# The two weight products of a graph layer, as three 16-bit products of high and low parts

## The chip, the cores and the metric

The kernel runs on one core of a Trainium2 chip. The metric is device time in microseconds (us) of one execution of the whole kernel, the median of several runs.

## What is computed

Input are 625 rows of 768 values, 20,000 edges between the rows, and the weights of a graph network of two attention layers and of one transformer block with eight experts. Only the first graph layer matters here. Cut to that:

```python
x0  = layernorm(x)                          # 625 x 768
xl  = (x0 @ W1).reshape(625, 4, 256)        # W1: 768 x 1024   "xl1"
e   = leaky_relu(alpha_src[src] + alpha_dst[dst], 0.2)   # alpha: sums of xl with a row per head
out = segment_sum(xl[src] * softmax_over_edges_into_dst(e), dst) + b1
h   = relu(layer_norm(out)) + (x0 @ Wr1 + br1)           # Wr1: 768 x 1024   "res1"
```

All of it is float32. The softmax over edges is done densely: an edge count matrix, 625 x 625, says how often each source reaches each target, and log(count) is added to the scores.

## The kernel before, in words

The 625 rows are five tiles (T = 5) of P = 125 rows, numbered t, or d where they are targets of edges. 768 is KD = 6 blocks of 128, HC = 1024 is two banks of 512. Each engine has its own program, in order; they meet at semaphores. TensorE's outputs go to four PSUM slots of 1024 columns in the order of `item_plan`: product n may start when the owner of product n-4 ("A" ScalarE, "D" VectorE) has emptied it (`free`, `done`, `emptied_by`).

*Start.* SyncE loads the edges, x, W1 and Wr1 (3072 KB each, one DMA each, L465 and L466), then rows of biases and small columns (L468 to L474), one DMA after the other. VectorE takes the moments of each tile (L1021), GpSimd the inverse root (L591, L592), VectorE normalizes (L1038), TensorE transposes (L1507), and ScalarE (tiles 0, 2, 4) or VectorE (tiles 1, 3) copies the transpose to `aT6` in float32 (L753, L1073).

*Count loop.* For each d, TensorE makes xl1 of tile d (12 float32 products of 512 columns, L1519), then sums the edge counts: the edges are sorted by target and come in groups of 500, of which 8 to 10 touch a tile (44 in all, so the loop has a length read from a register). Per group TensorE does 4 pairs of float16 products, 512 and 113 columns (L1557, L1558), with one-hot rows that are built on the fly in a ring of 4 groups (`oh_dst`, `oh_src`). VectorE builds a group with one comparison of 4 x 125 columns (L1105) and three of 625 (L1108); ScalarE builds the fourth source row in two steps, the absolute difference to `distance` (L774), and relu(1 - distance) (L779), one buffer between them. VectorE and ScalarE may be 4 groups ahead of TensorE (`oh_used`). For the next d they start when TensorE has left this count. VectorE first takes the sums of `xl1` with the attention rows (L1091, eight of 256 columns) and copies the counts out (L1115, L1119). GpSimd clamps the counts at 1 (L598), ScalarE takes the logarithm (L786), GpSimd makes the mask (L601).

*Attention.* 20 steps i (4 heads x 5 tiles), a pipeline over ScalarE (L837, exponential L842, copy of the transpose L753), VectorE (L1152, L1155, result L1177) and TensorE (transpose, product of 256 columns in float32). Between them TensorE does halves of res1 as `RES1_HALVES` says: tile 0 before the first step and in step 0, then (tile, half) (1,0) (1,1) (2,0) (2,1) in steps 1, 13, 15, 18, and tiles 3 and 4 behind the last step. W2 of the second layer is loaded at the end of the count loop and split into float16 high and low parts by ScalarE (L798) and VectorE (L1139), a half in step 7 and one in step 11 (`SPLIT_AT`). Behind it VectorE adds up each row tile (L1207, L1210, L1215), TensorE transposes it and multiplies by W2 and Wr2, already in the form "three products of float16 parts": high x high, high x low, low x high (`PARTS`, L1621 and L1519).

The rest (second layer, attention with 12 heads, experts) is not touched but for where buffers lie.

## Time and profile before

| | |
|---|---|
| median of 3 runs | 1099.87 us (1098.56 to 1102.97) |
| the profiled execution's own time | 1102.97 us, span 1101.2 us |
| TensorE busy | 1037.7 us, 94% of the span |
| VectorE, ScalarE, GpSimd busy | 729.8, 570.8, 184.9 us |
| granted TensorE clock, mean over the span | 0.978 |

The span is the time from the first to the last instruction of the profiled execution; it was also the slowest of the three runs. In the profile PE is TensorE's products, PEld its weight loads, DVE VectorE, ACT ScalarE, POOL GpSimd, SP SyncE. A line number is that of the statement that issued the instruction, and that can be a helper's: L1519 stands for all of `product`, L753 for all of `copy`. A duration of a product counts its way through the array, so a row of products is read by the distance of starts or by a merged row's length, not by the mean of one.

### The profile page before, as it was taken

To read this page: it belongs to the slowest core of one execution; us is meant where nothing else is said; L and a number is where in the kernel's file an instruction comes from. 1 tells how busy PE (TensorE), PEld (TensorE's weight loads), DVE (VectorE), ACT (ScalarE), POOL (GpSimd) and SP (SyncE) were. 2 spreads that over 40 slices of the span, in tenths; PEclk is the share of its full clock that TensorE was granted. 3 is DMA by queue.
4 is the path that set the end of the run, shared out by engine and by line. 5 is a ranking of instruction groups with operands and counts; after the bars stand their busy time and mean duration, and the time that the engine had idled before them with its cause. 6 is when DMAs were issued, how large, how long until landed. Compare 5 with 4: busy or idle time off the path is not lost.

```text
span 1101.2 us, 19073 instructions
## 1 busy us (share of the span) xinstructions
PE 1037.7 (94%) x6167; PEld 651.7 (59%) x6168; DVE 729.8 (66%) x1300; ACT 570.8 (52%) x782; POOL 184.9 (17%) x186
## 2 busy tenths in 40 slices
PE   5999999999999999989998699999999999999997
PEld 3555558756766775566777255555555555555554
DVE  6677768595666654189976888911129898989411
ACT  2666769513240344178834576811128778777310
POOL 3000040040205331072001301110103120211000
PEclk9999999999999999989998699999999999999999
DMA  8300030301507500030026699940009999999100
GB/s 312 106 0 0 1 115 1 115 1 59 112 1 156 87 1 1 1 112 2 2 86 201 244 390 325 351 168 0 25 0 352 375 375 360 390 359 390 72 4 3
DMA packets 92263, 155.60 MB, mean 141 GB/s; under 512 B 36507, under 2 KB 36587, under 8 KB 92214
## 3 DMA queue, kind: packets, MB, share of 16 engines
q1 hardware_dynamic: 89814, 149.20, 39.2%
q0 software_dynamic: 2400, 5.77, 1.5%
q8 instruction: 29, 0.48, 0.2%
q14 instruction: 20, 0.16, 0.0%
HBM read 153.21 MB, written 7.77 MB: 146 GB/s over the span
## 4 chain that ended last, share of the span: by engine, by line
PE 75%; DVE 10%; issue 5%; ACT 4%; DMA 2%; POOL 1%; DVEq 1%; SPq 0%; ACTq 0%; POOLq 0%
PE psum L1519 29%; PE psum L1794 18%; PE psum L1769 17%; PE psum L1778 2%; PE psum L1507 2%; PE psum L1557 2%; DVE area L1380 2%; DMA low<-in_L_ffn_W_dram 2%; DVE smalls L1021 1%; PE psum L1765 1%; PE psum L1677 1%; DVE area L1351 1%; DVE area L1108 1%; ACT low L915 1%; PE psum L1621 1%
## 5 line engine op out<-in xcount | busy, mean ns | idle before, releaser
L1380 DVE TENSOR_TENSOR area<-low,area 128x1536 f16<-128x1536 f32 x144 | 245.9, 1753 | 13.3 <-ACT area L970 13.1
L1519 PE MATMUL psum<-area,low 128*125 128x512 f16 (+4 forms) x1068 | 236.9, 381 | 1.3 <-DVE low L1253 1.3
L1769 PE MATMUL psum<-area,low 128*128 128x512 f16 x972 | 220.7, 381 | 0.0
L1794 PE MATMUL psum<-area,low 128*128 128x384 f16 x1296 | 219.3, 327 | 0.0
L970 ACT ACTIVATE area<-low 128x1536 f16<-128x1536 f32 x138 | 200.3, 1484 | 34.0 <-DMA low<-in_L_ffn_W_dram 28.1
L1519 PE MATMUL psum<-area 125*128 125x64 f16 (+10 forms) x1452 | 196.1, 289 | 10.1 <-DVE area L1351 5.5
L1519 PEld LDWEIGHTS psum<-area,low 128*125 128x125 f16 (+2 forms) x1068 | 136.4, 141 | 92.4 <-issue 53.1
L1794 PEld LDWEIGHTS psum<-area,low 128*128 128x128 f16 x1296 | 127.3, 98 | 80.7 <-issue 1.7
L1519 PEld LDWEIGHTS psum<-area 125*128 125x128 f16 (+3 forms) x1452 | 126.7, 122 | 62.8 <-issue 12.3
L1769 PEld LDWEIGHTS psum<-area,low 128*128 128x128 f16 x972 | 95.5, 98 | 113.9 <-issue 3.0
L981 ACT ACTIVATE low<-psum 128x512 f32<-128x512 f32 x54 | 31.9, 591 | 161.5 <-PE psum L1769 158.1
L1483 DVE TENSOR_TENSOR low<-psum,low 128x512 f16<-128x512 f32 x54 | 37.1, 687 | 107.9 <-ACT low L987 107.9
L1557 PE MATMUL psum<-area 125*125 x176 | 52.6, 394 | 9.8 <-issue 7.1
L693 POOL COPY low<-low 128x1 uint32 (+1 forms) x10 | 9.6, 959 | 309.8 <-DVE low L1401 309.8
L591 POOL TENSOR_SCALAR smalls<-smalls 125x1 f32<-125x1 f32 x20 | 14.4, 719 | 228.9 <-DVE smalls L1024 228.9
L779 ACT ACTIVATE area<-area,smalls 125x625 f16 x44 | 36.0, 818 | 22.6 <-PE psum L1558 15.9
L1105 DVE TENSOR_TENSOR area<-area 125x500 f16 x44 | 29.8, 678 | 23.5 <-PE psum L1558 15.6
L753 ACT ACTIVATE area<-psum 125x625 f32<-125x625 f32 (+3 forms) x42 | 27.8, 661 | 32.0 <-PE psum L1507 14.6
L774 ACT ACTIVATE area<-area 125x625 f16<-125x625 f16 x44 | 36.0, 819 | 14.8 <-ACTq L771 8.4
L1108 DVE TENSOR_SCALAR area<-area 125x625 f16 x132 | 42.6, 382 | 0.0
L915 ACT ACTIVATE low<-low,smalls 125x125 f32<-125x125 f32 (+4 forms) x60 | 36.4, 607 | 7.0 <-DVE smalls L1342 6.4
L987 ACT ACTIVATE low<-psum 128x512 f16<-128x512 f32 x54 | 32.0, 592 | 14.7 <-PE psum L1778 14.7
(246 smaller groups left out, 1183.9 us busy)
## 6 DMA issues: line engine op xcount, KB each, us to landing
low<-in_L_ffn_W_dram SPq DMA_DIRECT2D x144, 768.0 KB, 7.7
area<-in_L_gnn_W_dram SPq DMA_DIRECT2D x2, 3072.0 KB, 11.9
area<-in_L_gnn_Wr_dram SPq DMA_DIRECT2D x2, 3072.0 KB, 15.7
low<-in_x_dram SPq DMA_DIRECT2D x10, 336.0 KB
area<-in_L_ffn_Wv_dram SPq DMA_DIRECT2D x6, 384.0 KB, 6.2
area<-in_L_ffn_Wq_dram SPq DMA_DIRECT2D x6, 384.0 KB, 7.1
area<-in_L_ffn_Wk_dram SPq DMA_DIRECT2D x6, 384.0 KB, 6.1
area<-in_L_ffn_Wp_dram SPq DMA_DIRECT2D x2, 1152.0 KB, 6.7
```

Of the source, the lines that this page charges most:

```text
L774: act.activation(distance[:, 0:N], iota16[:, 0:N], ACT.Abs, scale=-1.0, bias=eT[:, 0, J - 1, bass.ds(lo + i, 1)]).then_inc(distance_ok[d], 1)
L779: act.activation(oh_src[:, bass.ds(i % AHEAD_G * (J * NP) + (J - 1) * NP, N)], distance[:, 0:N], ACT.Relu, scale=-1.0, bias=ones[0:P, 0:1] ...
L915: act.activation(abuf[i % ROWS][:, 0:w], abuf[i % ROWS][:, 0:w], ACT.Exp, scale=-1.0, bias=negm[:, i % 4:i % 4 + 1], accum_out=rsum[:, i % ...
L970: act.activation(unit_parts(u)[0], raw_view(u), ACT.Copy).then_inc(high_ok, 1)
L987: act.activation(hidT[c % 2][0], v3(psum[:, (2 + c % 2) * BANK:(3 + c % 2) * BANK], CK), ACT.Copy).then_inc(hidhi_ok, 1)
L1108: ins = dve.tensor_scalar(oh_src[:, bass.ds(i % AHEAD_G * (J * NP) + j * NP, N)], iota16[:, 0:N], eT[:, 0, j, bass.ds(lo + i, 1)], None, A ...
L1380: dve.tensor_tensor(low_, raw_view(u), high_, ALU.subtract).then_inc(low_ok, 1)
L1483: dve.tensor_tensor(hidT[c % 2][1], v3(psum[:, (2 + c % 2) * BANK:(3 + c % 2) * BANK], CK), hidT[c % 2][0], ALU.subtract).then_inc(hid_rel ...
L1519: ins = pe.matmul(place(name)[0:parts, at:at + w], left(q), right(q)[:, at:at + w], start=(q == 0), stop=(q == k - 1))
L1557: pe.matmul(low_, targets, oh_src[:, bass.ds(at, BANK)], start=False, stop=False)
L1769: ins = pe.matmul(psum[:, (c % 2) * BANK:(c % 2 + 1) * BANK], ht[x_][:, k, :], w1_s[c][w_][:, k, :], start=False, stop=(k == KD - 1 and x_ ...
L1794: ins = pe.matmul(psum[:, (4 + q) * BANK:(4 + q) * BANK + D // 2], hidT[c % 2][x_][:, j, :], w2_s[c][w_][:, j, q * D // 2:(q + 1) * D // 2 ...
```

## The change

- `x0T` takes the place of `aT6`: ScalarE writes the high float16 part of each transpose, VectorE the low part (transpose minus high), for all five tiles.
- W1 comes in six DMAs of 512 KB, into `g1_staged`. ScalarE makes `g1_parts[0]` = float16(64 x W1) block by block, between its copies of the transposes; VectorE makes `g1_parts[1]` = 64 x W1 - high, six instructions of 1024 columns, behind the last transpose and ahead of the count loop.
- xl1 and res1 are 36 float16 products of 512 columns per tile. Tile 0 of xl1 is written out so that it follows the split block by block (`by_x0_as_split`).
- Wr1 is loaded into the same `g1_staged` by one DMA when W1's low parts are done, and behind all of SyncE's early DMAs. GpSimd multiplies it by 64 in place (6144 columns), and, once the last xl1 is made, converts and subtracts it half by half: the first half ahead of its clamps of tiles 3 and 4, the second behind the masks.
- The factor 64 goes out again in the copies and additions behind the products.
- res1's order: (0,0) ahead of the first step, (1,0) in step 0, (2,0) in step 1, (0,1) (1,1) (2,1) in steps 13, 15, 18; tile 3 in two halves, tile 4 whole. `SPLIT_AT` moves to 8 and 12, and ScalarE waits there for Wr1's second half.
- `distance` has four buffers: ScalarE takes the difference for group i+1 ahead of its wait for group i's, and one more per d.
- The slots of several later weight buffers are exchanged (0 for 1).

```diff
-RES1_HALVES = {1: (1, 0), 13: (1, 1), 15: (2, 0), 18: (2, 1)}
+RES1_HALVES = {0: (1, 0), 1: (2, 0), 13: (0, 1), 15: (1, 1), 18: (2, 1)}
 ...
 @@ sync
-            sp.dma_start(w1_g, g_W1.rearrange("(k p) n -> p k n", p=128)).then_inc(w1g_in, 16)
-            sp.dma_start(wr1_g, g_Wr1.rearrange("(k p) n -> p k n", p=128)).then_inc(wr1g_in, 16)
+            for k in range(KD):
+                sp.dma_start(g1_staged[:, k, :], g_W1[k * 128:(k + 1) * 128, :]).then_inc(w1g_in[k], 16)
 ...
+            sp.wait_ge(w1_low, KD)
+            sp.dma_start(g1_staged, g_Wr1.rearrange("(k p) n -> p k n", p=128)).then_inc(wr1g_in, 16)
 @@ gpsimd
+            def residual_weights(q):
+                columns = slice(q * BANK, (q + 1) * BANK)
+                link(pool.tensor_copy(g1_parts[0][:, :, columns], g1_staged[:, :, columns]))
+                pool.tensor_tensor(g1_parts[1][:, :, columns], g1_staged[:, :, columns], g1_parts[0][:, :, columns],
+                                   ALU.subtract).then_inc(wr1_split, 1)
+            pool.wait_ge(wr1g_in, 16)
+            link(pool.tensor_scalar(g1_staged, g1_staged, SCALE_UP, None, ALU.mult))
+            for d in range(T - 2):
+                clamp(d)
+            done(pool, ("xl1", T - 1))
+            residual_weights(0)
+            for d in range(T - 2, T):
+                clamp(d)
             for d in range(T):
                 ...    # the masks
+            residual_weights(1)
 @@ scalar
-            for t in range(T):
-                if plan[item["x0T", t]][1] == "A":
-                    copy(("x0T", t), aT6[:, :, t * P:(t + 1) * P], tview(("x0T", t), KD, P))
+            for k in range(KD):
+                act.wait_ge(w1g_in[k], 16)
+                act.activation(g1_parts[0][:, k, :], g1_staged[:, k, :], ACT.Copy, scale=SCALE_UP).then_inc(w1_high, 1)
+                if k < T:
+                    done(act, ("x0T", k))
+                    act.activation(x0T[0][:, :, k * P:(k + 1) * P], tview(("x0T", k), KD, P), ACT.Copy).then_inc(x0_high, 1)
 ...
+                act.activation(distance[:, 0:N], iota16[:, 0:N], ACT.Abs, scale=-1.0,
+                               bias=eT[:, 0, J - 1, bass.ds(lo, 1)]).then_inc(distance_ok[d], 1)
                 with act.Fori(0, groups) as i:
                     act.wait_ge(src_act_ready[d], i + 1)
-                    act.activation(distance[:, 0:N], iota16[:, 0:N], ACT.Abs, scale=-1.0,
-                                   bias=eT[:, 0, J - 1, bass.ds(lo + i, 1)]).then_inc(distance_ok[d], 1)
+                    act.activation(distance[:, bass.ds((i + 1) % DISTANCES * NP, N)], iota16[:, 0:N], ACT.Abs, scale=-1.0,
+                                   bias=eT[:, 0, J - 1, bass.ds(lo + i + 1, 1)]).then_inc(distance_ok[d], 1)
 ...
                     if layer == 1 and i in SPLIT_AT:
+                        act.wait_ge(wr1_split, 2)
 @@ vector
+            def x0T_low(t):
+                columns = slice(t * P, (t + 1) * P)
+                dve.wait_ge(x0_high, t + 1)
+                emptied_by(("x0T", t), dve.tensor_tensor(x0T[1][:, :, columns], tview(("x0T", t), KD, P),
+                                                         x0T[0][:, :, columns], ALU.subtract))
 ...
+            for k in range(KD):
+                dve.wait_ge(w1_high, k + 1)
+                dve.scalar_tensor_tensor(out=g1_parts[1][:, k, :], in0=g1_staged[:, k, :], scalar=SCALE_UP,
+                                         in1=g1_parts[0][:, k, :], op0=ALU.mult, op1=ALU.subtract).then_inc(w1_low, 1)
 @@ tensor
+            def by_x0(name, t, c0, c1):
+                product(name, 3 * KD, lambda k: x0T[PARTS[k % 3][0]][:, k // 3, t * P:(t + 1) * P],
+                        lambda k: g1_parts[PARTS[k % 3][1]][:, k // 3, c0:c1], c1 - c0, P)
+            def by_x0_as_split(name):
+                ...
+                for w_, split_ in enumerate((w1_high, w1_low)):
+                    for k in range(KD):
+                        pe.wait_ge(split_, k + 1)
+                        for x_ in range(2 - w_):
+                            for at in (0, BANK):
+                                ins = pe.matmul(out_[0:P, at:at + BANK], x0T[x_][:, k, 0:P],
+                                                g1_parts[w_][:, k, at:at + BANK],
+                                                start=(w_ + k + x_ == 0), stop=(w_ == 1 and k == KD - 1))
 ...
-            pe.wait_ge(wr1g_in, 16)
-            by_x0(0, 0, BANK, False)
-            graph_attention(1, HEADS, HID, xl1, lambda: by_x0(0, BANK))
-            for t in range(3, T):
-                by_x0(t)
+            by_x0_half(0, 0)
+            graph_attention(1, HEADS, HID, xl1)
+            for t in range(3, T - 1):
+                for q in range(2):
+                    by_x0_half(t, q)
+            by_x0(("res1", T - 1), T - 1, 0, HC)
```

## Rows read from the trace of the kernel before

**Rows 1.** The page's chain that ended last, shares by engine.

```profile
PE 75%; DVE 10%; issue 5%; ACT 4%; DMA 2%; POOL 1%; DVEq 1%; SPq 0%; ACTq 0%; POOLq 0%
```

**Rows 2.** Stages: us of each engine busy (instructions), clock, DMA share, GB/s.

```profile
46.00:72.00 26.00, 23.44 (x111) 14.39 (x110) 18.80 (x57) 17.98 (x22) 1.21 (x1) 1.00 0.11 19
...
190.00:256.00 66.00, 66.00 (x252) 42.56 (x252) 51.09 (x88) 21.87 (x40) 13.36 (x10) 1.00 0.13 48
```

**Rows 3.** Chain of waits in order of time: start, us, what.

```profile
46.21 10.36 PE psum L1519 x24
...
66.58 0.42 PE psum L1557
...
68.42 0.42 PE psum L1557
...
266.93 7.80 PE psum L1519 x48
```

**Rows 4.** Timeline of TensorE: start, us, what [idle before].

```profile
22.45 12.03 PE L1519 MATMUL psum<-area,low 128*125 128x512 f32 x24
...
46.05 10.52 PE L1519 MATMUL psum<-area,low 128*125 128x512 f32 x24
...
71.83 10.52 PE L1519 MATMUL psum<-area,low 128*125 128x512 f32 x24
...
141.78 5.37 PE L1519 MATMUL psum<-area,low 128*125 128x512 f32 x12
```

**Rows 5.** Timeline of VectorE, count loop, tiles 0 and 1.

```profile
23.39 0.68 DVE L1105 TENSOR_TENSOR area<-area 125x500 f16 x1 [1.20 <-issue]
...
47.74 0.29 DVE L1119 TENSOR_TENSOR low<-low,smalls 125x125 f32<-125x125 f32 x1
...
49.62 0.68 DVE L1105 TENSOR_TENSOR area<-area 125x500 f16 x1 [1.59 <-issue]
...
51.09 0.68 DVE L1105 TENSOR_TENSOR area<-area 125x500 f16 x1
```

**Rows 6.** Groups by form: busy us, mean ns of one, idle before.

```profile
L1221 DVE TENSOR_TENSOR low<-psum,low 128x1000 f16<-128x1000 f32 x5 | 6.0, 1199 | 15.7 <-ACT low L811 15.7
...
L1139 DVE SCALAR_TENSOR_TENSOR area<-area 128x6144 f16<-128x6144 f32 x1 | 6.5, 6548 | 0.0
```

**Rows 7.** SyncE's last early issue, and time to landing of W1 and W2.

```profile
50.67 0.62 SPq L474 DMA_DIRECT2D smalls<-in_L_ffn_Wg_dram  x1
...
DMA to landing us min/median/max: 10.2/11.9/13.6
```

**Rows 8.** GpSimd's groups by form.

```profile
L606 POOL TENSOR_SCALAR area<-area x2: 6036/6064/6093, 476.1 to 489.0; 128x2304 f32<-128x2304 f32 x2
...
L607 POOL CAST area<-area 128x2304 f16<-128x2304 f32 x2 | 4.2, 2102 | 0.1
...
L608 POOL TENSOR_TENSOR area<-area 128x2304 f16<-128x2304 f32 x2 | 9.2, 4580 | 0.2
```

**Rows 9.** Timelines and instructions of GpSimd beside VectorE; one line's durations ns min/median/max.

```profile
70.80 2.02 POOL L598 TENSOR_SCALAR low<-low 125x625 f32<-125x625 f32 x1 [50.42 <-ACT low L763]
...
71.08 0.92 DVE L1091 CUSTOM_DVE_ANT_0 low<-area 125x256 f32<-125x256 f32 x1
...
363.10 3.90 POOL L629 TENSOR_TENSOR low<-low,area 125x768 f32<-125x768 f32 x2
...
363.25 2.08 DVE L1268 TENSOR_SCALAR low<-low,smalls 125x768 f32<-125x768 f32 x1 [2.81 <-POOL smalls L625]
...
L1038 DVE TENSOR_SCALAR low<-low,smalls x10: 625/674/2162, 13.0 to 392.0; 125x768 f32<-125x768 f32 x10
...
L601 POOL TENSOR_TENSOR low<-low x5: 1521/2064/2084, 147.2 to 154.2; 125x625 f32<-125x625 f32 x5
```

**Rows 10.** Timelines of TensorE and VectorE, end of the layer.

```profile
235.33 20.76 PE L1519 MATMUL psum<-area,low 128*125 128x512 f32 x48
...
249.84 3.50 DVE L1215 SCALAR_TENSOR_TENSOR area<-area 125x1024 f32<-125x1024 f32 x3
```

More of the change, by code:

```diff
@@ L32, in item_plan @@
     plan = [(("edges",), "D"), (("bounds",), "D")]
-    plan += [(("x0T", t), "AD"[t % 2]) for t in range(T)]
+    plan += [(("x0T", t), "D") for t in range(T)]
     for t in range(T):
@@ L45, in item_plan @@
             if i == 0:
+                plan += [(("res1", 0, 0), "A")] if layer == 1 else []
                 plan.append((("src_row", layer, 0), "A"))
-                plan += [(("res2", t), "A") for t in range(EARLY_RES2)] if layer == 2 else [(("res1", 0), "A")]
+                plan += [(("res2", t), "A") for t in range(EARLY_RES2)] if layer == 2 else []
             elif i % T == T - 2 and i // T + 1 < heads:
@@ L56, in item_plan @@
         if layer == 1:
-            plan += [(("res1", t), "D") for t in range(3, T)]
+            plan += [(("res1", t, q), "D") for t in range(3, T - 1) for q in range(2)] + [(("res1", T - 1), "D")]
     plan += [(name, "A" if name[0] == "hT" else "D") for name in NORM_ORDER]
@@ L153, in gnn_moe_kernel @@
         staged = A(5, 0, KH * D)
-        w2_parts, wr2_parts = parts(0, KH * D), parts(1, KH * D)
+        g1_parts = [v3(part, KD) for part in parts(0, KD * HC)]
+        w2_parts, wr2_parts = parts(1, KH * D), parts(0, KH * D)
         row_a = [A(2, 0, HC, P), A(2, HC, HC, P)]
@@ L173, in gnn_moe_kernel @@
         res1 = v3(A(4, 0, T * HC, P), T)
-        res1_early = [low[0:P, TW + 4 * N:TW + 4 * N + HC], T_[0:P, KD * N:KD * N + HC], A(2, T * HC, HC, P)]
-        assert 4 * N + HC <= XW and KD * N + HC <= TW
+        res1_early = [low[0:P, TW + 4 * N:TW + 4 * N + HC], T_[0:P, KD * (N + 1):KD * (N + 1) + HC], A(2, T * HC, HC, P)]
+        assert 4 * N + HC <= XW and KD * (N + 1) + HC <= TW
         row_a2 = [A(2, 4096, D, P), A(2, 4096 + D, D, P)]
-        wv_parts, wk_parts, wp_parts = (parts(s, KD * D) for s in (0, 1, 1))
-        res2_early = [A(0, KD * D + t * D, D, P) for t in range(EARLY_RES2)]
+        wv_parts, wk_parts, wp_parts = (parts(s, KD * D) for s in (1, 0, 0))
+        res2_early = [A(1, KD * D + t * D, D, P) for t in range(EARLY_RES2)]
         assert KD * D + EARLY_RES2 * D <= SW
@@ L595, in _, with clamp @@
                 inverse_root(t, t + 1)
-            for d in range(T):
+            def clamp(d):
                 pool.wait_ge(absent_ok, d + 1)
                 pool.tensor_scalar(counts[:, d, :], counts[:, d, :], 1.0, None, ALU.max).then_inc(clamped, 1)
+            def residual_weights(q):
[11 more added lines that the diff above has]
+                clamp(d)
             for d in range(T):
@@ L790, in _, with residual_copy @@
             logs(T - 1, T)
+            def residual_copy(t, q):
+                done(act, ("res1", t, q))
+                emptied_by(("res1", t, q), act.activation(res1_early[t][:, q * BANK:(q + 1) * BANK],
+                                                          place(("res1", t, q), BANK, P), ACT.Copy, scale=1.0 / SCALE_UP))
             def xl2_copy(t):
@@ L831, in _ @@
                         if i == 0:
+                            if layer == 1:
+                                residual_copy(0, 0)
                             source_row(0)
@@ L843, in _ @@
                                        accum_out=rsum[:, q]).then_inc(exp_ok, 1)
-                    if layer == 1 and i == 2:
-                        copy(("res1", 0), res1_early[0], place(("res1", 0), HC, P))
                     if layer == 1 and i in SPLIT_AT:
+                        act.wait_ge(wr1_split, 2)
                         q = SPLIT_AT.index(i)
@@ L849, in _ @@
                     if layer == 1 and i - 2 in RES1_HALVES:
-                        t, q = RES1_HALVES[i - 2]
-                        copy(("res1", t, q), res1_early[t][:, q * BANK:(q + 1) * BANK], place(("res1", t, q), BANK, P))
+                        residual_copy(*RES1_HALVES[i - 2])
                     if layer == 2 and i == 2:
@@ L1591, in graph_attention @@
                         by_x0_half(*RES1_HALVES[i])
-            def by_x0(t, first=0, width=HC, whole=True):
-                product(("res1", t), KD, lambda k: aT6[:, k, t * P:(t + 1) * P], lambda k: wr1_g[:, k, :], width, P,
-                        first, whole)
-            pe.wait_ge(wr1g_in, 16)
-            by_x0(0, 0, BANK, False)
-            graph_attention(1, HEADS, HID, xl1, lambda: by_x0(0, BANK))
-            for t in range(3, T):
-                by_x0(t)
+            by_x0_half(0, 0)
+            graph_attention(1, HEADS, HID, xl1)
+            for t in range(3, T - 1):
+                for q in range(2):
+                    by_x0_half(t, q)
+            by_x0(("res1", T - 1), T - 1, 0, HC)
             pe.wait_ge(g_low, 2)
```

70 lines of the change are left out of this document (44 added, 26 removed).

## The prediction

> **What bounds the kernel now.** I read the page's chain of waits first, to see which engine ends last: TensorE has 75% of it [rows 1]. Then the stages. In the count loop of a tile TensorE is busy 23.4 us of 26, in the last stretch of the first layer 66.0 of 66 [rows 2]. So the first layer is bound by TensorE's order of work, and other engines matter where they make it wait. The layer lies in front of all else; what it gains or loses moves the rest of the span as a block.
>
> Three views of the count loop say more. The chain shows the float32 product of a tile at 10.36 us for 24 records, and then single products of groups that start 1.84 us apart [rows 3] (66.58, 68.42). A group's four pairs need about 1.2 us; the rest is between the groups, "issue" in the timeline, and the same for all groups behind the fifth. The first five come at 1.1 us each, because they were built during the product. From product to product, starts 46.05 and 71.83, a tile with 10 groups takes 25.8 us [rows 4]; tiles 2 to 4 go until 141.78, 23.9, 23.9 and 22.1 us for 9, 9 and 8 groups. VectorE builds a group in 1.47 us (49.62 to 51.09) and starts 3.6 us behind the start of the product, since it must first copy the count out (ends 48.0) [rows 5].
>
> **The change part by part.** Own time of the profiled execution: 1102.97 us; the median is 3.1 us lower, and I take 3.1 us off at the end.
>
> *The products.* The later layer already does this form: 24 products of 512 and 24 of 256 columns in 7.80 us [rows 3], 0.423 ns a column. 36 products of 512 columns are then 7.8 us, against 10.36: 2.56 us less for each of ten (xl1 and res1 of five tiles), 25.6 us of TensorE's work. How much counts depends on the place.
>
> *Start.* VectorE ended its copies at 22.2 (its first group starts at 23.39 with 1.20 of issue before it) [rows 5]. Now it has five low parts where it had two copies. 1000 columns of this kind took 1.20 us [rows 6], so 750 are 0.93. The three more, and the waits for ScalarE's high parts, push the last normalization and transpose back by 1.7 us to about 24.4; ScalarE's copy 0.8, the last low part 0.93: 26.1. Then six low parts of W1: 6144 columns took 6.55 us [rows 6], so 32.6. ScalarE's six conversions, about a microsecond each, lie between its copies, where it waits for transposes; what they hide behind is VectorE, and if they were late, the low parts would be. TensorE follows block by block and ends xl1 of tile 0 at about 33.2, a little ahead of before (22.45 plus 12.03, 34.5, [rows 4]). But no group is built by then. VectorE starts at 33.8, the first group is there at 35.4, TensorE takes it at 35.8 and goes on at 1.85 us each: 35.8 + 7 x 1.85 + 1.25 = 50.0, against 46.05. Plus 4.0 us.
>
> *Tiles 1 to 4.* The product's end no longer decides, since VectorE is late: 3.6 us until it starts, 1.56 for the first group, 0.45 until TensorE has it, 5.6 us behind the product's start. With 10 groups: 5.6 + 9 x 1.85 + 1.25 = 23.5, against 25.8. 2.3 us less for each of four tiles: minus 9.2. ScalarE had 2.04 us per group, two steps of 0.82 with waits between; the four distance buffers take out the wait for its own result, about 0.25 us. It is not ahead of TensorE by less than before, so I give them nothing of their own. If ScalarE's chain were what spaces the groups, it would be another 0.1 to 0.2 us for each of 36 groups, up to 6 us less. Count loop so far: minus 5.2.
>
> *GpSimd's part of Wr1.* SyncE issues its last early DMA at 50.67 [rows 7]; with 3 MB less in front, at the rate of some 400 GB/s (3072 KB in 7.7 us, my estimate from W1's landing), that is about 43. SyncE's new wait, for W1's low parts, is over at 32.6, and behind it in its queue is only W2's load at 142. Wr1 lands some 10.2 us after its issue [rows 7]: 54. Then GpSimd multiplies 6144 columns in place: 2304 took 6.06 us, so 16.2 us, 54 to 70, in the middle of tile 1's groups. The halves are a conversion (2304 in 2.10: 3072 in 2.8) and a subtraction (4.58: 6.1), 8.9 us each [rows 8], the first from the end of the last xl1 (about 125), the second behind the masks, in the first steps of attention.
>
> Does this cost VectorE? No row shows a GpSimd instruction beside the group building, but there are rows for each kind. A VectorE normalization of 768 columns takes 0.63 to 0.67 us (minimum and median of ten); at 363.25 one took 2.08 us and the next 2.16, the maximum, while GpSimd had two additions of two tensors, 3.90 us together [rows 9]. VectorE waited 1.4 to 1.5 us of GpSimd's 1.95, some 75 to 80%. From the other side, the masks' subtractions take 1.52 us at best and 2.06 in the median, where scores are computed beside them [rows 9]. But beside GpSimd's clamp, an instruction with one tensor and a constant like the new multiplication (2.02 us), one VectorE sum of 256 columns started at 71.08 and took 0.92 where its neighbours took 0.42, and the next ones ran free [rows 9]: 0.5 of 2.02, a quarter. That sum reads two tensors; three of the four comparisons of a group read one, as the normalization does. The nearest row in kind is the normalization. I take 80%: 13 us for the multiplication. VectorE is 1 us ahead of TensorE then, which leaves 12. Bounds: 0 and 16.2 less 1. GpSimd's new waits, for Wr1 and for the last xl1, hold back only its own clamps.
>
> *First half of Wr1*, beside tile 4's groups: 80% of 8.9 is 7.1; 1 us is covered by groups already built: plus 6 (0 to 8). TensorE's first res1 waits for nothing, it comes behind the count. The clamps of tiles 3 and 4 come later, but the masks are needed only when the scores are.
>
> *Second half*, beside scores of steps 1 to 4: 7.1 us of VectorE again. Half of res1 and two ready steps cover 2: plus 5 (0 to 7). ScalarE's new wait in step 8 is met long before. Behind it would be the exponentials of all later steps.
>
> *res1 in attention.* The half ahead of the first step and the one in step 1 are in the chain: 1.3 us less each, 2.6. Seven more halves lie where TensorE is always busy: 9.0 us. But VectorE must have joined row tile 0 before TensorE can transpose it. It did its three joins from 249.84, the first until 251.1, while TensorE was at res1 until 256.1 [rows 10]: with TensorE 9.0 us earlier and VectorE only by the 2.6 us that lie ahead of step 16, VectorE ends last and 7.4 us are left. Sum: minus 10.0.
>
> *Nothing*: 0.1 us of clearing a column on GpSimd at the start (idle there); the factor 1/64 within copies that are there anyway; the exchanged slots; tile 3's addition in two instructions, beside TensorE's products (0.2 us, and shown if VectorE ends last).
>
> Sum: +4.0 - 9.2 + 12 + 6 + 5 - 10.0 = +7.8 us. 1102.97 + 7.8 - 3.1 = 1107.7, so 1108 us.
>
> What the Trainium skill says of this: its page "SBUF — State Buffer", section "Who interferes with whom", has VectorE and GpSimd share one port pair, held by one of them for its whole instruction, and names among VectorE's users those with two inputs in SBUF and the fast forms of copy and tensor_scalar. The rows on the normalization agree (2.08 against 0.63); the sum of 256 columns beside the clamp does not (0.92 against 0.42, with the clamp going on for 1.2 us more). By the page VectorE would stand still for the full 16.2 and twice 8.9 us, which is the second case below.
>
> **The rivals.** *Held for the whole length*: the 20% that short instructions leave free are a fixed 0.3 us at head and tail, and a long one blocks throughout: 15 + 8 + 7, minus 15.2: +14.8, 1115 us. For it: 0.4 us free in the additions can be head and tail. Against: the clamp row.
>
> *The multiplication lets VectorE through* as the clamp did, a quarter: 16.2 x 0.25 = 4, less 1, the other two as forecast: 3 + 6 + 5 - 15.2 = -1.2, 1099 us. For it: the same kind of instruction on the same type. Against: the groups' comparisons are not the sum of that row.
>
> *On the other side: no blocking worth the name*, because group building has 0.4 us of slack per group (1.47 against 1.85) and four groups of lead: from where a block is under 4 us VectorE catches up. -15.2: 1085 us. For it: a tile's loop has 3 us of such slack. Against: at 54 there is no lead, tile 1's first group is being built.
>
> *TensorE's clock*: granted 1.00 throughout these stages [rows 2], 2.4 GHz. A stop of 10 us could lower it; the first product of tile 0 took 12.03 against 10.52 us [rows 4] after a thin stretch, so 1.5 us on top. It is in the range only.
>
> **How the numbers follow.** Forecast 0.33, whole length 0.22, multiplication lets through 0.25, no blocking 0.20. Range 1087 to 1117; the forecast's own range is 1102 to 1113. A measurement of this kernel tells about 0.5% (5.5 us) from no change. Slower by more: whole length, 0.7 of the forecast, a little of the third: 0.50. Within: 0.22. Faster by more: the last, and a third of the third: 0.28.
>
> **What would show it.** L1519's merged row of tile 1 to 4 at 7.8 us; the first group product of tile 0 at about 36; starts of these products 21.6 to 23.5 us apart where GpSimd is idle. One comparison of VectorE between 54 and 70 with a duration of many us: held. GpSimd's multiplication and VectorE's groups side by side at 0.3 and 0.6 us: I am wrong, and the kernel is faster. Wrong too if Wr1 lands much later than 54 (beside tile 2, with a lead of four groups, the block costs 7 us less), or if the groups come faster than 1.85 us.

## The result, and the profile after

The changed kernel takes 1119.89 us (median of 4 runs, 1117.65 to 1121.45), the kernel before 1100.05 beside it (1098.56 to 1102.97, 4 runs): ratio 1.0182, 95% interval 1.0165 to 1.0199. Forecast were 1108 us and a range of 1087 to 1117. "Slower" came true; the size did not, 7.8 us forecast and some 20 measured. The profiled run took 1119.22 us with a span of 1117.5 (before 1102.97 and 1101.2).

First the page's chain by engine, to be held against [rows 1], and the stages (us of each engine busy with its instructions, then TensorE's granted clock, DMA share and GB/s; compare [rows 2]). The stages are tile 1 and tile 4 of the count loop, the start of attention up to its third exponential, and the rest of the layer.

```profile
PE 71%; DVE 13%; issue 6%; ACT 4%; DMA 2%; DVEq 1%; POOL 1%; ACTq 0%; SPq 0%; POOLq 0%
```

```profile
49.97:88.22 38.25, 23.09 (x123) 15.82 (x121) 34.62 (x58) 16.89 (x23) 18.01 (x2) 0.82 0.12 49
131.31:157.83 26.52, 20.44 (x106) 13.46 (x105) 24.47 (x50) 16.71 (x21) 11.17 (x3) 0.87 0.00 0
157.83:182.56 24.73, 18.31 (x95) 13.16 (x94) 19.73 (x24) 10.63 (x16) 20.18 (x8) 0.92 0.35 128
182.56:276.17 93.61, 88.21 (x454) 70.69 (x453) 75.38 (x157) 49.29 (x81) 13.36 (x10) 0.96 0.10 35
```

In the two tiles VectorE, the third figure, is "busy" for 34.6 of 38.3 us and for 24.5 of 26.5, and TensorE for 23.1 and 20.4: the bound has changed engines. How much of that is work shows the timeline of VectorE and GpSimd (start, us, engine, line, operation), first VectorE's:

```profile
53.55 0.96 DVE L1153 TENSOR_SCALAR area<-area 125x625 f16 x3
54.43 0.67 DVE L1150 TENSOR_TENSOR area<-area 125x500 f16 x1
55.02 16.47 DVE L1153 TENSOR_SCALAR area<-area 125x625 f16 x3
...
139.24 9.25 DVE L1153 TENSOR_SCALAR area<-area 125x625 f16 x3
...
159.15 1.06 DVE L1173 TENSOR_SCALAR low<-smalls 125x125 f32<-125x125 f32 x5
...
171.63 9.27 DVE L1173 TENSOR_SCALAR low<-smalls 125x125 f32<-125x125 f32 x5
```

And GpSimd's, same columns:

```profile
55.35 15.97 POOL L619 TENSOR_SCALAR area<-area 128x6144 f32<-128x6144 f32 x1 [33.25 <-DMA area<-in_L_gnn_Wr_dram]
...
139.32 2.91 POOL L614 CAST area<-area 128x3072 f16<-128x3072 f32 x1 [9.99 <-PE psum L1574]
142.31 6.00 POOL L615 TENSOR_TENSOR area<-area 128x3072 f16<-128x3072 f32 x1
...
170.99 3.31 POOL L614 CAST area<-area 128x3072 f16<-128x3072 f32 x1
174.38 6.04 POOL L615 TENSOR_TENSOR area<-area 128x3072 f16<-128x3072 f32 x1
```

Three comparisons that take 0.96 us took 16.47, and 9.25 the second time; five source diagonals of 1.06 us took 9.27. Each begins and ends within 0.7 us of GpSimd's work: 15.5 of 15.97 us lost, 8.3 of 8.99, 8.2 of 9.43. The first is the sign that the prediction had named for "held", a comparison of many us. Last the starts of TensorE's products, against [rows 4], and the end of the layer, against [rows 10]:

```profile
24.17 7.59 PE L1611 MATMUL psum<-area,low 128*125 128x512 f16 x32
...
49.97 7.94 PE L1574 MATMUL psum<-area,low 128*125 128x512 f16 x36
...
71.90 0.68 PE L1634 MATMUL psum<-area 125*125 x1 [12.62 <-DVE area L1153]
...
88.22 7.94 PE L1574 MATMUL psum<-area,low 128*125 128x512 f16 x36
...
255.44 15.71 PE L1574 MATMUL psum<-area,low 128*125 128x512 f16 x72
271.56 1.05 PE L1562 MATMUL psum<-smalls,area 125*128 125x125 f32 x8 [0.42 <-issue]
274.47 1.90 PE L1562 MATMUL psum<-smalls,area 125*128 125x125 f32 x8 [1.87 <-DVE area L1257]
```

The product takes 7.94 us (7.8 forecast); the tile around it grew from 25.8 to 38.3, and TensorE stood still for 12.62 of them, released by VectorE's comparison.

One table for the versions: us between landmarks of the profiled runs' timelines (start of the span, products' starts in the count loop, end of the counts, first and third exponential, first product of the second weights), and the median of each version's runs. g2, which has another order at the end of the counts, is told below.

```
                        tile 0   tile 1  tiles 2,3  tile 4  to exp 1  exp 1-3  rest of layer   median
before                   46.05    25.78    47.87    22.08    11.17     7.06      98.05         1100
after                    49.97    38.25    43.09    26.52     9.85    14.88      93.61         1119.9
e1 no multiplication     49.72    23.36    43.06    26.52     9.85    14.89      91.99         1103.6
e2 twelve pieces         49.83    23.37    43.83    26.52     9.84    14.90      91.90         1105.0
f2 six pieces            49.90    28.84    43.12    26.51     9.85    14.90      91.97         1107.8
f3 two pieces            49.74    37.82    43.07    26.52     9.85    14.88      91.98         1116.0
f1 all in pieces         49.96    25.28    45.17    26.32     9.85     9.47      91.81         1100.7
e3 no work on Wr1        49.33    23.43    42.99    19.65     9.85     6.67      91.75         1087.5
e4 ScalarE and VectorE   49.62    23.35    43.82    21.67    10.86     5.48      94.46         1092.7
g1 the same, old plan    49.53    23.33    43.86    21.67    10.86     5.87      92.06         1090.3
e8 before, one dose      44.65    37.40    47.67    21.97    11.27     7.06      98.04         1110.5
g3 before, two doses     44.82    52.93    47.67    21.96    11.28     7.07      98.03         1127.6
e5 before, distances     45.88    25.80    47.87    22.08    11.28     5.88      99.22         1100.5
```

### The profile page after: what moved, and what is told of

The parts are those of the page before. It is cut to its first block, busy times and chain, and to the rows that moved or that the text cites. A ratio compares the mean times of both kernels' runs of the same rounds, so it can differ in the third digit from the quotient of the medians.

```text
span 1117.5 us, 19451 instructions
## 1 busy us (share of the span) xinstructions
PE 1022.0 (91%) x6287; PEld 660.2 (59%) x6288; DVE 770.7 (69%) x1310; ACT 575.0 (51%) x796; POOL 216.5 (19%) x192
## 4 chain that ended last, share of the span: by engine, by line
PE 71%; DVE 13%; issue 6%; ACT 4%; DMA 2%; DVEq 1%; POOL 1%; ACTq 0%; SPq 0%; POOLq 0%
PE psum L1574 24%; PE psum L1867 18%; PE psum L1842 17%; PE psum L1634 3%; DVE area L1153 3%; PE psum L1562 2%; PE psum L1851 2%; DMA low<-in_L_ffn_W_dram 1%; DVE area L1435 1%; ACT low L955 1%; PE psum L1838 1%; DVE smalls L1061 1%; PE psum L1750 1%; DVE low L1173 1%; PE psum L1694 1%
## 5 line engine op out<-in xcount | busy, mean ns | idle before, releaser
L1574 PE MATMUL psum<-area 125*128 125x64 f16 (+10 forms) x1452 | 198.7, 291 | 10.5 <-DVE area L1406 4.4
L1574 PE MATMUL psum<-area,low 128*125 128x512 f16 (+3 forms) x1152 | 201.9, 335 | 1.4 <-DVE low L1308 1.3
L1574 PEld LDWEIGHTS psum<-area,low 128*125 128x125 f16 (+1 forms) x1152 | 134.9, 129 | 63.9 <-DVE low L1308 1.6
L1634 PE MATMUL psum<-area 125*125 x176 | 58.9, 426 | 29.7 <-DVE area L1153 21.8
L1153 DVE TENSOR_SCALAR area<-area 125x625 f16 x132 | 66.2, 558 | 0.0
L1634 PEld LDWEIGHTS psum<-area 125*125 x176 | 25.6, 145 | 46.2 <-issue 39.5
L812 ACT ACTIVATE area<-area,smalls x44 | 35.5, 807 | 32.8 <-PE psum L1635 32.8
L1027 ACT ACTIVATE low<-psum 128x512 f16<-128x512 f32 x54 | 32.0, 592 | 14.7 <-PE psum L1851 14.7
L1635 PE MATMUL psum<-area 125*125 x176 | 39.4, 224 | 0.0
L1406 DVE TENSOR_TENSOR area<-psum,area 125x125 f16<-125x125 f32 (+4 forms) x60 | 33.0, 550 | 9.0 <-ACT area L948 6.2
## 6 DMA issues: line engine op xcount, KB each, us to landing
area<-in_L_gnn_Wr_dram SPq DMA_DIRECT2D x2, 3072.0 KB, 10.3
```

What stands on the lines that cost most here:

```text
L812: act.activation(oh_src[:, bass.ds(i % AHEAD_G * (J * NP) + (J - 1) * NP, N)], distance[:, bass.ds(i % DISTANCES * NP, N)], ACT.Relu, scal ...
L1153: ins = dve.tensor_scalar(oh_src[:, bass.ds(i % AHEAD_G * (J * NP) + j * NP, N)], iota16[:, 0:N], eT[:, 0, j, bass.ds(lo + i, 1)], None, A ...
L1406: emptied_by(("attT", i - 2), dve.tensor_tensor(lo_[:, 0:k, 0:P], tview(("attT", i - 2), k, P, P), hi_[:, 0:k, 0:P], ALU.subtract))
L1574: ins = pe.matmul(place(name)[0:parts, at:at + w], left(q), right(q)[:, at:at + w], start=(q == 0), stop=(q == k - 1))
L1634: pe.matmul(low_, targets, oh_src[:, bass.ds(at, BANK)], start=False, stop=False)
L1635: ins = pe.matmul(high, targets, oh_src[:, bass.ds(at + BANK, N - BANK)], start=False, stop=False)
```

## The experiments

The theory after the result, A: each of GpSimd's long instructions shuts VectorE out for its whole length, and VectorE is what the count loop now hangs on. Rivals: a partial loss as forecast (B), and the load of Wr1, which lands in the same stretch (C).

**e1, no multiplication.** With e2, e3 and e8 on one chip, beside 14 runs of before (1100.70).

```diff
-            link(pool.tensor_scalar(g1_staged, g1_staged, SCALE_UP, None, ALU.mult))
```

> The changed kernel without GpSimd's multiplication of Wr1 by 64 (so the residual product comes out 64 times too small; everything else, the load of Wr1 at the same time among it, is kept). Theory A, GpSimd's instruction shuts VectorE out for its whole length: tile 1's stretch (product to product, 38.25 us in the changed kernel, 25.8 before) falls by 15.5 to 18 us to 20.5 to 22.5, VectorE's three comparisons at its place take 0.96 us in place of 16.47, and the kernel takes 1102 to 1104.5 us. Theory B, the share forecast (80% of 16.2 us less 1 us): 1107 to 1108. Theory C, the load of Wr1 that lands in the same stretch is what slows it: 1118 to 1120.

Measured: 1103.61 us (10 runs, 1101.69 to 1107.12), ratio 1.0033 [1.0019, 1.0047]. Tile 1 takes 23.36 us, 14.9 less. The time is A's, and B and C fall; the stretch stays 0.9 us above A's. VectorE's own rows show why 14.9 and not 15.5:

```profile
57.69 0.97 DVE L1152 TENSOR_SCALAR area<-area 125x625 f16 x3
59.46 0.68 DVE L1149 TENSOR_TENSOR area<-area 125x500 f16 x1 [0.80 <-PE psum L1634]
```

In the whole tile VectorE waits once, 0.80 us. A stop takes that wait away, and nothing else: 15.5 less 0.8 is 14.7, near the 14.9.

**e2, the multiplication in twelve pieces.**

```diff
-            link(pool.tensor_scalar(g1_staged, g1_staged, SCALE_UP, None, ALU.mult))
+            for k in range(KD):
+                for q in range(2):
+                    piece = g1_staged[:, k, q * BANK:(q + 1) * BANK]
+                    link(pool.tensor_scalar(piece, piece, SCALE_UP, None, ALU.mult))
```

> The changed kernel with the multiplication in twelve instructions of 512 columns in place of one of 6144, each waiting for the one before. Theory A with the lock let go at each instruction's end: VectorE gets in about one operation between two pieces, twelve in 16.5 us, where a group of edges needs four; some 3 of the stretch's groups are passed, and the stretch costs about 5 us less than with one instruction: 1113 to 1117. If the lock is not let go between instructions that stand behind each other, or if twelve starts cost more than they let through: 1119 to 1122. Theory C, the load: 1118 to 1120.

Measured: 1104.99 us (5 runs, 1102.07 to 1109.37), ratio 1.0051 [1.0023, 1.0080]: outside every case that I had written. The same arithmetic on the same engine at the same time costs 1.4 us more than none at all, by intervals that overlap; in the table it is 0.8 us, all of it in tiles 2 and 3. GpSimd's twelve, then VectorE:

```profile
54.87 21.28 POOL L622 TENSOR_SCALAR area<-area 128x512 f32<-128x512 f32 x12 [32.88 <-DMA area<-in_L_gnn_Wr_dram]
```

```profile
56.71 1.31 DVE L1156 TENSOR_SCALAR area<-area 125x625 f16 x3
57.94 0.67 DVE L1153 TENSOR_TENSOR area<-area 125x500 f16 x1
58.53 1.31 DVE L1156 TENSOR_SCALAR area<-area 125x625 f16 x3
```

A piece takes 1.77 us of GpSimd and 0.35 of VectorE (1.31 for 0.96). A group grows from 1.47 to 1.82 us, just under TensorE's 1.84 ([rows 3]), so it costs tile 1 nothing (23.37 us).

**f2 and f3, six and two pieces** (`for k in range(KD)` over rows of 1024 columns; two halves of 3072). One run each.

> The changed kernel with the multiplication in six instructions of 1024 columns. Theory S with a hold in proportion (0.35 us for 512 columns): 0.7 us for a piece, no comparison over 1.1 us, one time of 1103 to 1107. If the hold sets in as a whole between 512 and 1024 columns: a comparison beside each piece takes up to 2.7 us, the stretch 33 to 38 us, 1114 to 1120.

> The changed kernel with the multiplication in two instructions of 3072 columns. In proportion to 0.35 us for 512 columns: 2.1 us for a piece, 1104 to 1109. If instructions of this size hold VectorE for their whole length, as the cast of 3072 columns did: one comparison of some 8 us beside each, 1117 to 1120.

Measured: 1107.76 and 1116.0 us. VectorE's rows of f2, then f3:

```profile
60.08 2.35 DVE L1154 TENSOR_SCALAR area<-area 125x625 f16 x3
```

```profile
56.24 16.44 DVE L1155 TENSOR_SCALAR area<-area 125x625 f16 x3
```

Six pieces (17.15 us in all, 2.86 each) take 1.39 us of VectorE each, 0.83 at the start and 0.56 at the end of a piece, with operations at their usual length between. Two pieces (16.06 in all) take 15.5: each holds one comparison for 8.1 us, and only the first of these gets done at the gap between them. So neither of my two rules for f2, 0.7 or 2.7 us, was right; f3 is the second case in its rows (two comparisons of some 8 us), and its time of 1116.0, a single run, lies 1 us below that case's.

What a piece leaves free is about the same time for 512 columns (1.42 us), 1024 (1.47) and the clamp's 625 ([rows 9]: 2.02 less 0.50, 1.52). That does not make a rule: a piece of 3072 leaves 0.3 us and the whole of 6144 leaves 0.5. And 1.47 us is also what a group of VectorE takes by itself: with pieces of 512 and 1024 columns, one piece of GpSimd goes by for one group, in step. What decides how long VectorE is let through stays open.

**f1, the casts and subtractions in pieces too.** The twelve multiplications are those of e2. Beside 17 runs of before (1100.41).

```diff
+                for k in range(KD):
+                    link(pool.tensor_copy(g1_parts[0][:, k, columns], g1_staged[:, k, columns]))
+                    ins = pool.tensor_tensor(g1_parts[1][:, k, columns], g1_staged[:, k, columns],
+                                             g1_parts[0][:, k, columns], ALU.subtract)
```

> The changed kernel with all of GpSimd's work on Wr1 in instructions of 512 columns: twelve multiplications, and in each half six casts and six subtractions in turn, each waiting for the one before. The twelve-piece run took VectorE 0.35 us for a piece (one comparison of 0.73 us among those of 0.38) in place of the whole length. Theory S, what an instruction of GpSimd takes from VectorE depends on its size, so the casts and subtractions let VectorE through in pieces too: tile 4's stretch falls from 26.5 to 19.7 to 21 us, the step from the first exponential to the third from 14.9 to 6.7 to 8.5, the kernel takes 1088 to 1093 us. Theory K, it depends on the kind (a tensor_scalar of 32-bit columns gives way, a cast or a subtraction of two tensors does not, as the masks' subtraction, 625 columns, holds VectorE's 2.0 us operations for 1.2 us): 24 pieces hold for about 1.2 us each where VectorE is at work, 1096 to 1106.

Measured: 1100.67 us (12 runs, 1097.33 to 1104.33), ratio 1.0003 [0.9990, 1.0017]: in K's range, and S falls. Tile 4 gains nothing (26.32 for 26.52), the first exponentials gain 5.4 us (9.47 for 14.9). GpSimd in tile 4, and a group of VectorE there:

```profile
133.37 1.15 POOL L616 TENSOR_TENSOR area<-area 128x512 f16<-128x512 f32 x1
134.47 0.70 POOL L615 CAST area<-area 128x512 f16<-128x512 f32 x1
135.25 1.47 POOL L616 TENSOR_TENSOR area<-area 128x512 f16<-128x512 f32 x1
```

```profile
131.55 3.16 DVE L1158 TENSOR_SCALAR area<-area 125x625 f16 x3
134.62 1.08 DVE L1155 TENSOR_TENSOR area<-area 125x500 f16 x1
135.62 3.16 DVE L1158 TENSOR_SCALAR area<-area 125x625 f16 x3
```

A group of VectorE takes 4.07 us (131.55 to 135.62) for 1.47, beside two pairs of cast and subtraction that last 4.07: 1.3 us lost to a pair of 2.0. Over the six pairs four groups take 14.2 us for 5.9, 8.3 lost, just what the whole instructions took. In the count loop the size helps the multiplication alone; beside the source diagonals and the first scores it helped the casts and subtractions too. Smaller ones were not tried. Tile 1 took 1.9 us more than in e2 with the same instructions there. VectorE's comparisons, by threes, in that tile:

```profile
58.65 1.66 DVE L1158 TENSOR_SCALAR area<-area 125x625 f16 x3
...
60.81 1.66 DVE L1158 TENSOR_SCALAR area<-area 125x625 f16 x3
```

They lose 0.70 us where e2's lost 0.35, a group takes 2.16 us, more than TensorE's 1.84, and the twelve pieces last 24.13 us in place of 21.28. So the price of a piece of 512 columns is 0.35 or 0.70 us in two kernels that do the same in this tile, and why stays open.

**e3, none of GpSimd's work on Wr1.**

```diff
-            link(pool.tensor_scalar(g1_staged, g1_staged, SCALE_UP, None, ALU.mult))
-            residual_weights(0)
+            pool.sem_inc(wr1_split, 1)
-            residual_weights(1)
+            pool.sem_inc(wr1_split, 1)
```

> The changed kernel without any of GpSimd's work on Wr1: no multiplication, no two casts, no two subtractions; the residual products read W1's halves in their place, so their values are W1's, at the same cost to TensorE. Theory A with all pieces on the path: 15.5 to 18 us for the multiplication, 8 for the first half in tile 4's stretch, 8 to 8.5 for the second half beside the source diagonals of head 1: 1084 to 1090. The forecast's sizes (12, 6, 5): 1096 to 1098. If only the multiplication is on the path: 1102 to 1104.

Measured: 1087.54 us (4 runs, 1086.54 to 1088.44), ratio 0.9881 [0.9863, 0.9900]. All three pieces are on the path: from e1 to e3 another 16.1 us, 6.9 of it in tile 4 and 8.2 between the first and the third exponential. Everything else in the change is worth 12.5 to 13.2 us; the forecast had 15.2. The rows of the group's first comparison (busy us, mean ns, idle before and its releasers) of before, after and e3, in this order, show what the shorter product did to VectorE:

```profile
L1105 DVE TENSOR_TENSOR area<-area 125x500 f16 x44 | 29.8, 678 | 23.5 <-PE psum L1558 15.6 <-issue 7.8
```

```profile
L1150 DVE TENSOR_TENSOR area<-area 125x500 f16 x44 | 29.6, 674 | 7.7 <-issue 6.6 <-PE psum L1635 0.8
```

```profile
L1149 DVE TENSOR_TENSOR area<-area 125x500 f16 x44 | 29.8, 677 | 9.3 <-issue 6.6 <-PE psum L1634 2.4
```

VectorE waited 15.6 us for TensorE in before's five loops. The 16-bit products alone (e3) leave 2.4 of it: the time that they took from TensorE is the cover that GpSimd's work would have needed.

**e8 and g3, one and two doses in the kernel before.** A dose is one multiplication of Wr1 by 1.0 on GpSimd; TensorE waits for it ahead of res1, long after its end. g3 has a second such instruction in front.

```diff
+            pool.wait_ge(wr1g_in, 16)
+            pool.wait_ge(counted, 1)
+            pool.tensor_scalar(wr1_g, wr1_g, 1.0, None, ALU.mult).then_inc(wr1_done, 1)
             for d in range(T):
                 pool.wait_ge(absent_ok, d + 1)
 ...
```

> The kernel before with one thing added: GpSimd multiplies Wr1 (6144 columns of 32 bits, in place) by 1.0 once tile 0's counts are ready, near 50 us, with no transfer near it and all of before's 32-bit products kept. Theory A: tile 1's stretch grows by 15.5 to 18 us, the kernel takes 1115 to 1118. Theory B: plus 12, 1112. Theory C: 1099 to 1102. If the two bounds on TensorE's products matter (VectorE's work ahead by four groups at 16 us), the dose may come out near 14: 1114.

Measured: 1109.92, 1110.53 and 1112.65 us, and a fourth run of 6104 us that is not of this kernel's kind and that no run here explains; ratio of the three 1.0103 [1.0077, 1.0129]. Their median is 9.8 us above before (10.9 if the fourth is counted, 1111.59, as the expectation of g3 has it), and C falls. A's number misses by 4.5 us. B's is near, its rows aren't: the dose, 15.78 us from 46.88, stopped VectorE for more than 80%.

```profile
48.29 13.17 DVE L1108 TENSOR_TENSOR area<-area 125x500 f16 x1 [1.58 <-issue]
61.38 2.03 DVE L1111 TENSOR_SCALAR area<-area 125x625 f16 x3
```

Its first comparison lost 12.5 us and the next three 1.1, 13.6 together. In before VectorE waits for TensorE in this tile, once it is four groups ahead:

```profile
54.61 0.97 DVE L1108 TENSOR_SCALAR area<-area 125x625 f16 x3
58.36 0.68 DVE L1105 TENSOR_TENSOR area<-area 125x500 f16 x1 [2.77 <-PE psum L1558]
```

13.6 less 2.8 is 10.8. The table has 11.6 us in tile 1, and 1.4 less in tile 0, ahead of the dose, where the first product took 10.88 us for 12.03. That made theory W, against a fixed share P:

> The kernel before with two GpSimd multiplications of Wr1 by 1.0 behind each other, where the run with one took 1111.6 us (10.9 more than before). Theory W, a blockade costs its length less what VectorE would have waited in that stretch (2.9 us, from 55.49 to 58.36 in the kernel before, used up by the first): the second costs its 15.8 us in full, 1126.5 to 1129. Theory P, a fixed share of the length is paid (10.9 of 15.8): 1121.5 to 1123.5.

Measured: 1127.58 us (4 runs, 1125.85 to 1128.66), ratio 1.0240 [1.0218, 1.0262] to 1100.8. The second dose costs 15.5 us in tile 1 (52.93 less 37.40), and VectorE lost 15.5 to it; by the medians it is 16 to 17. W holds, P with its 10.9 falls. GpSimd's two and the comparisons beside the second:

```profile
47.07 15.78 POOL L598 TENSOR_SCALAR area<-area 128x6144 f32<-128x6144 f32 x1 [26.80 <-DVE low L1123]
62.94 15.72 POOL L599 TENSOR_SCALAR area<-area 128x6144 f32<-128x6144 f32 x1
```

```profile
61.58 17.54 DVE L1112 TENSOR_SCALAR area<-area 125x625 f16 x3
```

**e4, ScalarE and VectorE split Wr1.** The full computation. The low half of a row of 1024 is written over the row's own first half, the high half over the second half of the row two before; rows 0 and 1 use spare columns and are copied back. The highs stand behind ScalarE's loops (rows 0 and 1 behind loop 1, 2 and 3 behind 2, 4 and 5 behind 3), the lows behind `attention_values` of tiles 1 to 4.

```diff
+                for k in HIGH_AT.get(d, ()):
...
+                    act.activation(r1_part(k, 0, True), g1_staged[:, k, :], ACT.Copy, scale=SCALE_UP).then_inc(r1_high, 1)
...
+                for k in LOW_AT.get(d, ()):
+                    dve.wait_ge(r1_high, k + 1)
+                    dve.scalar_tensor_tensor(out=r1_part(k, 1), in0=g1_staged[:, k, :], scalar=SCALE_UP,
+                                             in1=r1_part(k, 0, True), op0=ALU.mult, op1=ALU.subtract).then_inc(wr1_split, 1)
```

> The changed kernel with no work on Wr1 on GpSimd at all, and the full computation: ScalarE writes the high halves of Wr1's six rows of 1024 columns behind loops 1, 2 and 3, VectorE the low halves in place behind loops 1 to 4 (1.2 us each, and two copies of 0.3 us); W2's parts, V's, K's and the projection's go back to the places they have in the kernel before. The run with no such work at all took 1087.5. If the added 7.8 us of VectorE and 6 us of ScalarE lie beside TensorE's products (VectorE has 3.7 us free in each of the stretches of 21.5): 1087 to 1090. If they lie on the path in full: 1094 to 1096. Rival, the order of VectorE's queue (each low half waits for ScalarE's high half, and the counts' copy behind it is waited for by the clamp): 1090 to 1094.

Measured: 1092.73 us (6 runs, 1090.68 to 1094.09), ratio 0.9928 [0.9912, 0.9943]: faster than both kernels, 5 us above e3. That is the rival's range, the order of VectorE's queue. Tiles 1 and 2 take the added work at no cost, tiles 3 and 4 pay 0.8 and 2.0 us, and the rest of the layer 2.7. VectorE's last low half and copies:

```profile
136.26 1.23 DVE L1162 SCALAR_TENSOR_TENSOR area<-area 128x1024 f16<-128x1024 f32 x1
137.52 0.89 DVE L1167 COPY area<-low 128x512 f32<-128x512 f32 x2
```

They stand ahead of the counts' copy, and TensorE's next product starts 0.69 us late behind them.

**g1 and g2, the plan of before; the last low halves later.** g1 (beside 17 runs of before, 1100.8):

```diff
-RES1_HALVES = {0: (1, 0), 1: (2, 0), 13: (0, 1), 15: (1, 1), 18: (2, 1)}
+RES1_HALVES = {1: (1, 0), 13: (1, 1), 15: (2, 0), 18: (2, 1)}
-            plan += [(("res1", t, q), "D") for t in range(3, T - 1) for q in range(2)] + [(("res1", T - 1), "D")]
+            plan += [(("res1", t), "D") for t in range(3, T)]
 ...
```

The part left out puts tile 0's second half behind the source row and its copy into step 2.

> The version that splits Wr1 on ScalarE and VectorE (1092.7 us), with the residual products and accumulators planned as in the kernel before: tile 0's product whole with its second half behind the source row, tiles 3 and 4 whole, halves for tiles 1 and 2. Theory H, tile 3's halves made the second turn of h1T wait 2.9 us: both turns stand together again, from the first behind-row to the first product of h1T 2 to 3 us less, 1089.5 to 1091. Theory V, VectorE's row of joins is the bound there and the turn only waits in its shadow: 1092 to 1094.

Measured: 1090.28 us (4 runs, 1090.02 to 1092.24), ratio 0.9910 [0.9889, 0.9931]. The total is H's (1089.5 to 1091), the place is not. The end of the layer:

```profile
227.59 15.70 PE L1576 MATMUL psum<-area,low 128*125 128x512 f16 x72
243.72 2.16 PE L1564 MATMUL psum<-smalls,area 125*128 125x125 f32 x16 [0.43 <-issue]
247.18 7.98 PE L1696 MATMUL psum<-area,low 128*125 128x512 f16 x48 [1.29 <-DVE area L1265]
```

Both turns stand together again, and a new wait of 1.29 us for VectorE stands behind them. From the last products' start to the first one of the second weights it is 19.6 us, 19.9 in e4, 20.7 after, 22.7 before: VectorE ends this stretch. The 2.1 us that g1 gains lie between the third exponential and 195 us; I have no row that says which edit of the plan gives them.

g2 moves one low half from loop 3 to 4, the last and the two copies behind `source_diagonals(1, 0)`, and the source row ahead of the first residual product.

```diff
                 source_diagonals(layer, 0)
+                if layer == 1:
+                    residual_lows(T)
 ...
```

> As the run before it in this list, and the last low halves later: one of VectorE's low halves of stretch 3 moved to stretch 4, the last and the two copies behind head 0's source diagonals, where VectorE waits 5 us for the source row's copy; the source row goes ahead of the first residual product on TensorE. If the low halves behind loops 3 and 4 cost 0.8 and 1.3 to 2 us, as the stretches say: 1.5 to 2.5 us less than the run before it, 1087 to 1089. If the later residual product (8 us ahead of the first turn of the exponentials) takes that back: no difference.

Measured: 1091.6 us (6 runs, 1086.58 to 1093.55), ratio 0.9908 [0.9885, 0.9931]: not to be told from g1, the second case. The first exponential comes 1.8 us earlier, the third 0.6, the second weights 0.5.

**e5, the four distance buffers alone, in the kernel before.**

```diff
-                    act.activation(distance[:, 0:N], iota16[:, 0:N], ACT.Abs, scale=-1.0,
-                                   bias=eT[:, 0, J - 1, bass.ds(lo + i, 1)]).then_inc(distance_ok[d], 1)
+                    act.activation(distance[:, bass.ds((i + 1) % DISTANCES * NP, N)], iota16[:, 0:N], ACT.Abs, scale=-1.0,
+                                   bias=eT[:, 0, J - 1, bass.ds(lo + i + 1, 1)]).then_inc(distance_ok[d], 1)
```

> The kernel before with the four distance buffers alone, and one distance computed ahead of the loop. As forecast, nothing: the groups' period stays 1.84 us, 1099.5 to 1101.5. Rival: ScalarE's two steps back to back take 1.43 us and free the groups' period down to VectorE's 1.47 us, some six groups of 0.37 in each of five loops, 1089 to 1093.

Measured: 1100.45 us (12 runs, 1098.67 to 1102.84), ratio 0.9997 [0.9984, 1.0011]. Nothing, as forecast; tile 1 takes 25.80 us.

## Why the prediction was wrong

The failed step is the size of what GpSimd's work takes from VectorE, "I take 80%: 13 us for the multiplication. VectorE is 1 us ahead of TensorE then, which leaves 12", and the same 80% twice more: VectorE lost 97% of the multiplication (15.5 of 15.97 us), and 14.9 us were paid for it. A second step failed in the arithmetic, the 10.0 us of res1. The mechanism, its place (54 forecast, 55.35 measured; 16.2 us, 15.97) and its direction were right. Term by term:

- *Start*, +4.0: +3.9. SyncE issued Wr1 at 44.96, forecast 43.
- *Shorter products in tiles 1 to 4*, -9.2: -9.6 (tile 1 from e1, tile 4 from e3), and -4.8 against -4.6 in tiles 2 and 3 of the changed kernel itself.
- *Multiplication*, +12: +14.9 in its stretch, 16.3 by the medians of after and e1. Of the difference 1.6 us are in the rest of the layer of the profiled run (93.61 for 91.99), where its clock was granted 0.96 for e1's 0.97. f3 stopped VectorE just as long and has 91.98 there, so no run shows that the multiplication costs these 1.6.
- *First half*, +6: +6.9. *Second half*, +5: +8.2. Two ready steps and half of res1 were to cover 2 us of it; the row at 171.63 shows source diagonals, not scores, being stopped, and behind them TensorE without work. They covered nothing.
- *res1 in attention*, -10.0: in e3 -1.3, -0.4 and -6.3, so -8.0. In the changed kernel itself the last part is -4.4. At the end VectorE is the bound, which the forecast had, but its sum counts 2.6 us twice. By its own rows VectorE's first join would end 2.6 us earlier, at 248.5, where TensorE had ended res1 at 256.1: 7.6 us in all, the 2.6 among them, and not 7.4 on top of them. e3's 8.0 is near that. Of g1's 6.0 behind the third exponential, 3.1 are in the last stretch and 2.9 before it.
- *Distance buffers*, 0: 0 (e5).
- *Tile 3's halves*, taken at nothing: nothing that can be shown; the wait of 1.87 us at 274.47 is new and was not foreseen, but g1 without it gains 0.3 us there.

The sum to the second weights' first product is +18.1 us against +7.8; the span behind it came out 1.8 us shorter. Of the 10.3 between the two sums 2.9 are the multiplication's stretch, 0.9 and 3.2 the two halves, 3.9 the shortfall of res1 (10.0 less 6.1; 2.4 by the double count), less some 0.5 gained in the first terms. The final 12 us also hold 3.6 by which the profiled runs lie off their medians (before's 2.9 above, after's 0.7 below).

## What to carry to other kernels

A long instruction put on GpSimd beside a busy VectorE cost about its length here (14.9 us for 15.97, 15.5 for 15.7), less the time that VectorE would have waited in that stretch (2.8 us in e8); count this wait in the version after the change, since a shorter product on TensorE takes it away (15.6 us before, 2.4 with the 16-bit products). If the work must go there, try a tensor-and-constant operation in pieces of 512 columns (0.35 us of VectorE each in e2, 0.70 in f1), and price it by what a row of the same length lost, not by a share from a row of another length. Otherwise give it to engines whose queues have gaps: here ScalarE and VectorE did it for 5 us (e4 against e3; g1 is 3 above e3, with another plan) where GpSimd took 32.

## What the runs showed of the hardware that I had not expected

GpSimd's multiplication on 32-bit columns in place, beside VectorE's 16-bit comparisons, by columns of an instruction: 512, 0.35 us of 1.77 lost to VectorE in e2 and 0.70 of some 2.1 in f1; 1024, 1.39 of 2.86; twice 3072, 15.5 of 16.06; 6144, 15.5 of 15.97. A cast and a subtraction of 512 columns together: 1.3 of 2.0.

TensorE's clock after such a stop: granted 1.00 in tile 1 of e1 and 0.82 after. TensorE had been idle from 59.3 to 71.9; the next two groups run at 0.53 us for a pair where others take 0.28, at a granted clock of 0.50, the lower of its two levels (1.2 of 2.4 GHz), until 76.2. That is 2 us more for the two groups, and the stretch does not show them, since VectorE's groups come 1.47 us apart behind the stop and TensorE catches up.
